# Block 1's second tile of attention: weights as two fp16 halves instead of one fp32 stationary operand

## The chip, the cores and the metric

The kernel runs on one core of one Trainium2 chip. The metric is the device time in microseconds (us) of one execution, and the median of several executions is compared. Engines are named as in the profile: PE is TensorE (PEld its weight loads), DVE is VectorE, ACT is ScalarE, POOL is GpSimd, SP is the engine that issues most of the transfers.

## The reference

One block of a small language model over 2 x 1024 tokens with a vocabulary of 128 and a width of 512, all in fp32. What matters here:

```python
h = tok(x)                                     # embedding, rms norm, projection, rms norm
h = h + attn(layernorm(h), wq, wk, wv, wo)     # 32 query heads, 8 key/value heads, head size 16, causal
h = h + ffn(layernorm(h), w_gate, w_up, w_down)   # silu(gate) * up, hidden size 2048

att = softmax(mask(q @ k.T / sqrt(16)))        # over all earlier positions
y   = att @ v
```

## The kernel before, in words

All tokens with the same id have the same query, key and value, so attention runs over the 128 ids of the vocabulary, each weighted with how often the id has been seen so far (`cT`, the counts). The 2048 tokens are 16 tiles of 128; two tiles make a block, so there are 8 blocks. A **unit** V is one tile and one key/value head group, that is 4 query heads: 8 units for a tile, 16 for a block, 128 in all. Block 1 has units 16 to 31, and its second tile has units 24 to 31.

A unit goes through these steps:

1. PE transposes two 128x128 pieces of the query rows (`turn`, L1009), and ACT (blocks 0 and 1) or DVE (later blocks) copies them to `Qst` (`stack`, L484 or L779).
2. PE computes the scores (L1020), and ACT the exponential into one of three buffers `E` (L508).
3. DVE multiplies it with the counts (L813, semaphore `w_rdy`).
4. PE multiplies with the values (`values`). The weights are the stationary operand and there are 4 of them, one for each head.

Step 4 has two forms. For V < `WIDE`, the fp32 weights in `E` are stationary against `Vf` (16 values and a one, 17 columns of fp32, L1038), two slots after the unit's scores. For V >= `WIDE`, ACT makes an fp16 copy `WTh` of the weights (L518, `wt_hi`), an engine subtracts it from the fp32 weights into the fp16 remainder `WTl` (L369 on POOL, `wt_lo`), and PE multiplies both with `Va` (high and low halves of the values and a one, 33 columns of fp16), 8 matmuls (L1044, L1045), three slots after the scores. ACT then copies two units' results out of the bank (`PVs`, L530 for the fp32 form, L533 for the fp16 form). DVE takes reciprocals of the sums (L834), and POOL multiplies (L385), in the fp16 form after adding the high and low columns (L381).

Before the change `WIDE` is 32: blocks 0 and 1 take the fp32 form, blocks 2 to 7 the fp16 form.

The order on every engine is written out by hand. `phase(n, att, ffn, m)` runs the attention of block n beside the feed-forward layer of block m = n - 1, in 24 slots. In slot s of 0 to 15, PE does `score` of unit s of the block, `turn` of unit s + 1, `values` of an earlier unit, and `gate_up(m, s)`: 24 matmuls of 256 columns (L1066 to L1068) for 128 hidden features. In slot s, ACT does `stack`, tanh of hidden piece s - 1 (L500), exp of unit s (L508), the fp16 copy of the gated piece (L512, it waits for DVE's L806), then the fp16 weight copy of unit s - 1 if there is one (L518), the copy of a finished bank, and in block 1 one `split_high`. DVE does L801 and L806 of piece s - 1, L813 of unit s, the reciprocal in odd slots, and in block 1 one `split_low`. POOL does the fp16 remainder of the gated piece (L365), and then that of the weights. In slots 16 to 23 PE does the down projection (12 matmuls of 512 columns for each slot) and between them, for each tile of the attention block, the transposes of y (L1091), the output projection `wo` (L1099 to L1101), and the transposes of the normalized rows (L1106).

Block 1 has extra work. The feed-forward weights arrive as fp32 and are split there into fp16 halves, 24 pieces in all: ACT scales and copies the high half (L475, L476), and DVE computes the low half (L752 and L754 for pieces 0 to 15, one L757 for pieces 16 to 23). PE can do `gate_up(0, s)` only when piece s is split, and the down projection of slot 16 + q only when piece 16 + q is split. These are the slots in which ACT takes its halves, and DVE takes its own one slot later:

```python
HI_NEXT = {-1: 4, 0: 5, 1: 6, 3: 7, 4: 8, 6: 9, 7: 10, 8: 11, 9: 12, 11: 13, 12: 14, 13: 15, 14: 16, 15: 17, 16: 18, 17: 19, 18: 20,
           19: 21, 20: 22, 21: 23}
SECOND_SLOTS = dict(yt=(15, 20), wo=(16, 21), ln=(17, 21), xhat=(17, 21), xn=(19, 23), fetch=(18, 22), m=(22, 3))
# PE, in gate_up:          if m == 0: pe.wait_ge(split_lo, s + 1)
# PE, down projection:     pe.wait_ge(gt_lo, 2 * q + 2); pe.wait_ge(split_lo, 16 + q + 1)
```

So DVE splits piece 11 in slot 9, 12 in slot 10, none in slot 11, 13 in slot 12, 14 in slot 13, 15 in slot 14, 16 in slot 15, 17 in slot 16 and 18 in slot 17. In slot 17 DVE also does the layer norm of the first tile (L849 to L858) before piece 18.

Of the kernel before, what the change touches and what calls it, by code (L numbers as in the profile page):

```python
# [4 lines left out]
ALU = mybir.AluOpType  # L5
# [21 lines left out]
UPB = UPT * TPB  # L27
# [7 lines left out]
MROW = 48  # L35
RING = 3
VFW = HD + 1
WIDE = 2 * UPB

EPS_RMS, EPS_LN = 1e-6, 1e-5  # L40
NEG = -3.0e38
# [26 lines left out]
def lm_block(nc, x_col, embT, emb, nw, projT, wqkv, wo, ffn_w, out, tok_tab, l_tab0, l_tab1, g_tab0, g_tab1):  # L68
    ctx = ExitStack()
    with ctx:  # L70
        def sb(name, width, dt):
            return ctx.enter_context(nc.sbuf_tensor(name, [P, width], dt))

        def sem(name):
            return ctx.enter_context(nc.semaphore(name))
# [13 lines left out]
        E = [sb(f"weights{i}", GW, F32) for i in range(RING)]  # L89
        WT = sb("weights_split", 2 * RING * GW, F16)  # L90
        WTh, WTl = ([WT[:, (2 * r + i) * GW:(2 * r + i + 1) * GW] for r in range(RING)] for i in (0, 1))
# [99 lines left out]
        def pv_bank(pair):  # L191
            return f_bank[1] if pair < UPB // 2 and pair % 2 == 1 else b_PV

        def lag(V):
            return 2 if V < WIDE else 3

# [21 lines left out]
        wt_hi, wt_lo, pv_rdy, pv_ev = (sem(n) for n in ("wt_hi", "wt_lo", "pv_ready", "pv_evacuated"))  # L218
# [69 lines left out]
        def _(pool):  # L288
# [28 lines left out]
            def fetch_rows(t):  # L317
                k = t % TPB
                if t >= TPB:
                    pool.wait_ge(h1_rdy, t - TPB + 1)  # L320
                g.indirect_dma_start(out=QG[k][:, :].bitcast(F32), out_offset=None, in_=tok_tab,  # L321
                                     in_offset=bass.IndirectOffsetOnAxis(ap=idx_x[:, t:t + 1].bitcast(U32), axis=0)
                                     ).then_inc(rows_in[k], 16)
# [13 lines left out]
            def fetch_max(t):  # L337
                pool.wait_ge(m_rdy, t - TPB + 1)
                fetch_local(t)
                fetch_group(t)  # L340
# [17 lines left out]
            def phase(n, att, ffn, m):  # L358
                at = (FIRST_SLOTS, SECOND_SLOTS, LATER_SLOTS)[min(n, 2)]
                for s in range(SLOTS):  # L360
                    if ffn and 1 <= s <= HC:
                        j = s - 1
                        i = m * HC + j
                        pool.wait_ge(gt_hi, i + 1)
                        g.tensor_tensor(gtl[:, j, :], g2[j % 2], gth[:, j, :], ALU.subtract).then_inc(gt_lo, 1)  # L365
                    if att and 1 <= s <= UPB and n * UPB + s - 1 >= WIDE:
                        V = n * UPB + s - 1
                        pool.wait_ge(wt_hi, V + 1 - WIDE)
                        g.tensor_tensor(WTl[V % RING], E[V % RING][:, :], WTh[V % RING], ALU.subtract).then_inc(wt_lo, 1)  # L369
                    if att and n > 0 and 5 <= s < UPB + 5 and s % 2 == 1:  # L370
                        k, i = divmod((s - 5) // 2, 4)
                        t = n * TPB + k
                        pool.wait_ge(pv_ev, 4 * t + i + 1)
                        if t >= TPB:
                            pool.wait_ge(yt_rdy, t - TPB + 1)
                        w = 2 * REP * PVW
                        pv = PVs[k][:, i * w:(i + 1) * w].rearrange("p (h c) -> p h c", c=PVW)
                        yv = y[k][:, i * P:(i + 1) * P].rearrange("p (h d) -> p h d", d=HD)
                        num = pv[:, :, HD:2 * HD]
                        if 8 * t + 2 * i >= WIDE:  # L380
                            g.tensor_tensor(yv, pv[:, :, 0:HD], num, ALU.add).then_inc(num_rdy, 1)  # L381
                            pool.wait_ge(num_rdy, 4 * t + i + 1 - WIDE // 2)
                            num = yv
                        pool.wait_ge(rd_rdy, 4 * t + i + 1)
                        last = g.tensor_tensor(yv, num, rden[k][:, 8 * i:8 * i + 8].unsqueeze(2).broadcast_to([P, 8, HD]), ALU.mult)  # L385
                        if i == 3:
                            last.then_inc(y_rdy, 1)
                    for k in range(TPB):
                        t = n * TPB + k
                        if att and s == at["fetch"][k] and t + TPB < TILES:  # L390
                            if t + TPB == TILES // B:
                                pool.wait_ge(g_out[1], 16)
                                for i in range(4):
                                    pool.wait_ge(l_out[1][i], 16)
                            fetch_rows(t + TPB)
                            fetch_max(t + TPB)
            phase(0, True, False, 0)
            for n in range(1, BLOCKS):
                phase(n, True, True, n - 1)
            phase(BLOCKS, False, True, BLOCKS - 1)  # L400

        @block.scalar
        def _(actq):
# [82 lines left out]
            def phase(n, att, ffn, m):  # L486
                at = (FIRST_SLOTS, SECOND_SLOTS, LATER_SLOTS)[min(n, 2)]
                for s in range(SLOTS):
# [12 lines left out]
                    if att and s < UPB:  # L501
                        V = n * UPB + s
                        actq.wait_ge(scores, V + 1)
                        if V >= WIDE + RING:
                            actq.wait_ge(wt_lo, V - RING + 1 - WIDE)
# [61 lines left out]
        def _(dve):  # L567
            v = nc.vector
# [219 lines left out]
            def phase(n, att, ffn, m):  # L788
                at = (FIRST_SLOTS, SECOND_SLOTS, LATER_SLOTS)[min(n, 2)]
                for s in range(SLOTS):  # L790
# [17 lines left out]
                    if att and s < UPB:  # L808
                        V = n * UPB + s
                        t = n * TPB + s // UPT  # L810
                        dve.wait_ge(exp_done, V + 1)
                        w = E[V % RING][:, :].rearrange("p (h n) -> p h n", h=REP)
                        v.scalar_tensor_tensor(w, w, SEEN_MAX, cT[:, t * P:(t + 1) * P].unsqueeze(1).broadcast_to([P, REP, P]),  # L813
                                               ALU.min, ALU.mult).then_inc(w_rdy, 1)
                    if n == 0 and 3 <= s < UPB + 3 and s % 2 == 1:
                        k, i = divmod((s - 3) // 2, 4)
                        pair = 4 * k + i
                        dve.wait_ge(pv_rdy, 2 * pair + 2)
                        pv = pv_bank(pair)[:, 0:2 * REP * VFW].rearrange("p (h c) -> p h c", c=VFW)
                        v.reciprocal(rden[k][:, 8 * i:8 * i + 8], pv[:, :, HD]).then_inc(rd_rdy, 1)  # L820
                        dve.wait_ge(rd_rdy, pair + 1)
                        yv = y[k][:, i * P:(i + 1) * P].rearrange("p (h d) -> p h d", d=HD)
                        v.tensor_tensor(yv, pv[:, :, 0:HD], rden[k][:, 8 * i:8 * i + 8].unsqueeze(2).broadcast_to([P, 8, HD]),
                                        ALU.mult).then_inc(pv_ev, 1)
                        if i == 3:
                            dve.wait_ge(pv_ev, pair + 1)
                            v.tensor_scalar(st[:, 25:26], rden[k][:, 0:1], 1.0, None, ALU.mult).then_inc(y_rdy, 1)
# [61 lines left out]

            place_max(0)  # L890
            phase(0, True, False, 0)
            for n in range(1, BLOCKS):
                phase(n, True, True, n - 1)
            phase(BLOCKS, False, True, BLOCKS - 1)
            store_rows(TILES - 1)

# [304 lines left out]
```

## Time and profile before

| what | value |
|---|---|
| median of 3 runs | 745.5 us (745.23 to 746.47) |
| the profiled execution: its own time | 745.95 us |
| the profiled execution: span from first to last instruction | 744.2 us |
| busy share of the span: PE, DVE, ACT, POOL | 95%, 56%, 47%, 40% |
| mean granted TensorE clock | 0.96 of full speed |

The span is the time between the first and the last instruction on the core. The profiled execution took 1.75 us more than its span. Busy shares are averages over the whole kernel; block 1's phase, in which the change lies, runs from about 113 to 206 us of the span.

### The profile page before, as it was taken

The numbers are of one execution on the slowest core, as the hardware profiler recorded it, in microseconds if no ns is written. First come the engines' busy times: TensorE is split into PE (matmuls) and PEld (weight loads), VectorE is DVE, ScalarE is ACT, GpSimd is POOL, SyncE is SP. The second block draws the span as 40 slices with busy tenths as digits, with TensorE's granted clock in tenths as the row PEclk, the third lists the DMA queues.
The fourth block names the chain that finished last, engine by engine and source line by source line (L and its number), as shares of the span: only waits on it lengthen the run. The fifth ranks groups of instructions, "written<-read, shape, count | busy, mean of one in ns | idle before, by whom it ended". The sixth has DMA issues, their size and how long they took to land.

```text
span 744.2 us, 16126 instructions
## 1 busy us (share of the span) xinstructions
PE 705.3 (95%) x6268; PEld 539.3 (72%) x6268; DVE 415.3 (56%) x1038; ACT 351.6 (47%) x722; POOL 297.9 (40%) x402
## 2 busy tenths in 40 slices
PE   7639979999899999999999999999999999999998
PEld 4429858996389847985698659964997489857873
DVE  6875387777565546545565446564655465444320
ACT  6864336775256514652266316640565046521320
POOL 7020031223137543664266516753465437530220
PEclk9955699999999999999999999999999999999999
DMA  8959020001100011001100120003000210000000
GB/s 320 411 165 346 33 89 2 1 2 45 45 30 2 2 59 60 2 2 53 66 2 3 45 73 2 3 1 102 16 2 2 72 46 2 2 15 15 2 1 28
DMA packets 10458, 40.35 MB, mean 54 GB/s; under 512 B 1808, under 2 KB 2576, under 8 KB 8592
## 3 DMA queue, kind: packets, MB, share of 16 engines
q1 hardware_dynamic: 6912, 25.44, 8.9%
q0 software_dynamic: 3328, 13.11, 5.7%
q8 instruction: 50, 0.82, 0.5%
q10 hardware_dynamic: 144, 0.79, 0.3%
q14 instruction: 24, 0.20, 0.1%
HBM read 29.89 MB, written 9.44 MB: 53 GB/s over the span
## 4 chain that ended last, share of the span: by engine, by line
PE 88%; DVE 8%; ACT 2%; issue 1%; POOL 1%; DVEq 0%; POOLq 0%
PE banks L1066 14%; PE banks L1068 14%; PE banks L1067 14%; PE banks L1150 6%; PE banks L1152 6%; PE banks L1151 6%; PE banks L1038 5%; PE banks L1020 4%; PE banks L1009 2%; PE banks L1099 2%; PE banks L1101 2%; PE banks L1100 2%; PE banks L1044 1%; PE banks L1045 1%; PE banks L1091 1%
## 5 line engine op out<-in xcount | busy, mean ns | idle before, releaser
L1068 PE MATMUL banks<-xnT_and_h,ffn_weights 128*128 128x256 f16 x1024 | 279.2, 273 | 0.0
L1067 PE MATMUL banks<-xnT_and_h,ffn_weights 128*128 128x256 f16 x1024 | 279.1, 273 | 0.0
L1066 PE MATMUL banks<-xnT_and_h,ffn_weights 128*128 128x256 f16 x1024 | 279.0, 272 | 0.0
L365 POOL TENSOR_TENSOR gated_split<-gate_work,gated_split 128x256 f16<-128x256 f32 x128 | 86.4, 675 | 269.8 <-ACT gated_split L512 269.8
L369 POOL TENSOR_TENSOR weights_split<-weights,weights_split 128x512 f16<-128x512 f32 x96 | 111.0, 1156 | 0.0
L1066 PEld LDWEIGHTS banks<-xnT_and_h,ffn_weights 128*128 128x128 f16 x1024 | 100.9, 99 | 11.4
L1068 PEld LDWEIGHTS banks<-xnT_and_h,ffn_weights 128*128 128x128 f16 x1024 | 99.9, 98 | 11.8
L1067 PEld LDWEIGHTS banks<-xnT_and_h,ffn_weights 128*128 128x128 f16 x1024 | 99.9, 98 | 11.4
L500 ACT ACTIVATE gate_work<-banks,scales 128x256 f32<-128x256 f32 x128 | 60.5, 473 | 99.9 <-PE banks L1068 99.8
L813 DVE SCALAR_TENSOR_TENSOR weights<-weights,counts_T 128x512 f32<-128x512 f32 x128 | 87.6, 685 | 25.3 <-ACT weights L508 25.1
L508 ACT ACTIVATE weights<-banks,scales 128x512 f32<-128x512 f32 x128 | 87.2, 681 | 14.1 <-PE banks L1020 14.0
L801 DVE SCALAR_TENSOR_TENSOR gate_work<-gate_work,banks 128x256 f32<-128x256 f32 x128 | 52.9, 413 | 62.1 <-ACT gate_work L500 61.9
L512 ACT ACTIVATE gated_split<-gate_work 128x256 f16<-128x256 f32 x128 | 53.4, 417 | 68.3 <-DVE gate_work L806 68.3
L779 DVE COPY q_stack<-banks 128x256 f16<-128x256 f16 x96 | 27.8, 290 | 103.1 <-PE banks L1009 103.1
L1152 PE MATMUL banks<-ffn_weights,gated_split 128*128 128x512 f16 x224 | 85.0, 379 | 0.0
L1151 PE MATMUL banks<-ffn_weights,gated_split 128*128 128x512 f16 x224 | 85.0, 379 | 0.0
L1150 PE MATMUL banks<-ffn_weights,gated_split 128*128 128x512 f16 x224 | 84.9, 379 | 0.0
L321 POOL DMA_INDIRECT token_rows<-token_table,indices x16 | 15.7, 980 | 108.5 <-DVE xnT_and_h L849 95.3
L518 ACT ACTIVATE weights_split<-weights 128x512 f16<-128x512 f32 x96 | 58.9, 613 | 0.0
L806 DVE SCALAR_TENSOR_TENSOR gate_work<-banks,gate_work 128x256 f32<-128x256 f32 x128 | 54.3, 425 | 4.4
L552 ACT ACTIVATE xnT_and_h<-banks 128x512 f16<-128x512 f32 x16 | 9.6, 597 | 83.0 <-PE banks L1106 82.4
L1020 PE MATMUL banks<-q_stack,k_stack_even 128*128 128x128 f16 x256 | 44.6, 228 | 2.4 <-ACT q_stack L484 2.4
(235 smaller groups left out, 1110.4 us busy)
## 6 DMA issues: line engine op xcount, KB each, us to landing
ffn_weights<-in_ffn_w SPq DMA_DIRECT2D x12, 1024.0 KB, 15.5
out_rows_dram<-ffn_weights SPq DMA_DIRECT2D x16, 256.0 KB, 2.0
xnT_and_h<-in_wqkv SPq DMA_DIRECT2D x1, 1536.0 KB, 8.5
local_table<-gated_split SPq DMA_DIRECT2D x2, 640.0 KB, 4.9
local_table<-xnT_and_h SPq DMA_DIRECT2D x2, 640.0 KB, 3.6
gated_split<-in_projT SPq DMA_DIRECT2D x4, 256.0 KB, 4.0
ffn_weights<-in_wo SPq DMA_DIRECT2D x1, 1024.0 KB, 10.5
token_table<-weights_split ACTq DMA_DIRECT2D x1, 768.0 KB, 8.3
```

Of the source, the lines that this page charges most:

```text
L365: g.tensor_tensor(gtl[:, j, :], g2[j % 2], gth[:, j, :], ALU.subtract).then_inc(gt_lo, 1)
L369: g.tensor_tensor(WTl[V % RING], E[V % RING][:, :], WTh[V % RING], ALU.subtract).then_inc(wt_lo, 1)
L500: a.activation(th[j % 2], f_bank[j % 3][:, 0:BLK], ACT.Tanh, scale=c_tanh).then_inc(th_rdy, 1)
L508: a.activation(E[V % RING][:, :], b_S[V % 2], ACT.Exp, scale=c_exp).then_inc(exp_done, 1)
L813: v.scalar_tensor_tensor(w, w, SEEN_MAX, cT[:, t * P:(t + 1) * P].unsqueeze(1).broadcast_to([P, REP, P]), ALU.min, ALU.mult).then_inc(w_rd ...
L1020: last = t.matmul(b_S[V % 2][:, (2 * j + a) * P:(2 * j + a + 1) * P], (KstA, KstB)[a][:, gr * P:(gr + 1) * P], Qst[:, r * 256 + j * P:r * ...
L1066: t.matmul(o, wh, xTh[m % 2][:, c, :], start=c == 0, stop=False)
L1067: t.matmul(o, wh, xTl[m % 2][:, c, :], start=False, stop=False)
L1068: last = t.matmul(o, wl, xTh[m % 2][:, c, :], start=False, stop=c == DC - 1)
L1150: t.matmul(o, hh, dn_w(j, 0), start=j == 0, stop=False)
L1151: t.matmul(o, hh, dn_w(j, 1), start=False, stop=False)
L1152: last = t.matmul(o, hl, dn_w(j, 0), start=False, stop=j == HC - 1)
```

## The change

`WIDE` becomes 24, so units 24 to 31 take the fp16 form. Their high copy is made by ACT, as in later blocks. Their remainder is made by DVE instead of POOL, placed after L813 in the slot after the unit's scores, so in slots 9 to 16 of block 1. The values of these units move from slots 10 to 17 to slots 11 to 18, the copies of their banks on ACT go from slots 11, 13, 15, 17 to slots 12, 14, 16, 18 and are 264 columns wide instead of 136, and POOL gets one addition (L381) for each pair of units.

```diff
-WIDE = 2 * UPB
+WIDE = UPB + 8
+LOW_ON_DVE = 2 * UPB
...
@@ POOL, in phase
-                    if att and 1 <= s <= UPB and n * UPB + s - 1 >= WIDE:
+                    if att and 1 <= s <= UPB and n * UPB + s - 1 >= LOW_ON_DVE:
                         V = n * UPB + s - 1
                         pool.wait_ge(wt_hi, V + 1 - WIDE)
                         g.tensor_tensor(WTl[V % RING], E[V % RING][:, :], WTh[V % RING], ALU.subtract).then_inc(wt_lo, 1)
...
@@ DVE, in phase, after L813
+                    if att and 1 <= s <= UPB and WIDE <= n * UPB + s - 1 < LOW_ON_DVE:
+                        V = n * UPB + s - 1
+                        dve.wait_ge(wt_hi, V + 1 - WIDE)
+                        v.tensor_tensor(WTl[V % RING], E[V % RING][:, :], WTh[V % RING], ALU.subtract).then_inc(wt_lo, 1)
```

## Rows read from the trace of the kernel before

**Rows 1.** Page, part 1 and part 4: busy time by engine; the chain's shares by engine.
```profile
PE 705.3 (95%) x6268; PEld 539.3 (72%) x6268; DVE 415.3 (56%) x1038; ACT 351.6 (47%) x722; POOL 297.9 (40%) x402
...
PE 88%; DVE 8%; ACT 2%; issue 1%; POOL 1%; DVEq 0%; POOLq 0%
```

**Rows 2.** Windows of block 1's later slots and of its end: us, busy, PEclk.
```profile
142.10:169.90 27.80, 27.80 (x280) 25.87 (x277) 22.57 (x39) 21.14 (x46) 6.95 (x11) 1.00 0.01 2
199.20:206.40 7.20, 7.20 (x33) 3.39 (x34) 3.18 (x6) 0.60 (x1) 0.00 (x0) 0.81 0.01 3
```

**Rows 3.** Chain that ended last, slot 10 of block 1: start us, us, what.
```profile
149.74 0.22 PE banks L1020 x4
...
150.08 0.85 PE banks L1038 x8
150.93 0.12 PE banks L1066
153.56 0.22 PE banks L1020 x4
```

**Rows 4.** Chain that ended last, slots 6 and 7 of block 2: where each begins.
```profile
224.73 0.22 PE banks L1020 x4
...
227.89 0.22 PE banks L1020 x4
```

**Rows 5.** Timeline of DVE, slots 9 to 11 of block 1.
```profile
147.08 0.42 DVE L801 SCALAR_TENSOR_TENSOR gate_work<-gate_work,banks 128x256 f32<-128x256 f32 x1 [0.53 <-ACT gate_work L500]
...
150.90 0.42 DVE L801 SCALAR_TENSOR_TENSOR gate_work<-gate_work,banks 128x256 f32<-128x256 f32 x1 [0.38 <-ACT gate_work L500]
...
151.69 0.68 DVE L813 SCALAR_TENSOR_TENSOR weights<-weights,counts_T 128x512 f32<-128x512 f32 x1
152.29 1.23 DVE L752 SCALAR_TENSOR_TENSOR ffn_weights<-ffn_weights,scales 128x512 f16<-128x512 f32 x1
153.44 0.74 DVE L754 SCALAR_TENSOR_TENSOR ffn_weights<-ffn_weights,scales 128x512 f16<-128x512 f32 x1
154.71 0.42 DVE L801 SCALAR_TENSOR_TENSOR gate_work<-gate_work,banks 128x256 f32<-128x256 f32 x1 [0.53 <-ACT gate_work L500]
```

**Rows 6.** Timelines of ACT and POOL, slots 9 and 10 of block 1.
```profile
148.48 0.71 ACT L475 ACTIVATE ffn_weights<-ffn_weights,scales 128x512 f16<-128x512 f32 x1
149.09 0.71 ACT L476 ACTIVATE ffn_weights<-ffn_weights,scales 128x512 f16<-128x512 f32 x1
150.12 0.38 ACT L484 ACTIVATE q_stack<-banks 128x256 f16<-128x256 f16 x1 [0.32 <-PE banks L1009]
150.40 0.47 ACT L500 ACTIVATE gate_work<-banks,scales 128x256 f32<-128x256 f32 x1
...
151.81 0.42 ACT L512 ACTIVATE gated_split<-gate_work 128x256 f16<-128x256 f32 x1 [0.37 <-DVE gate_work L806]
...
152.30 0.67 POOL L365 TENSOR_TENSOR gated_split<-gate_work,gated_split 128x256 f16<-128x256 f32 x1 [2.33 <-ACT gated_split L512]
```

**Rows 7.** Timeline of ACT, slot 4 of block 2.
```profile
220.47 0.61 ACT L518 ACTIVATE weights_split<-weights 128x512 f16<-128x512 f32 x1
221.00 0.37 ACT L533 ACTIVATE pv<-banks 128x264 f32<-128x264 f32 x1
```

**Rows 8.** Chain, then DVE's timeline, slots 16 to 18 of block 1.
```profile
179.00 0.80 PE banks L1038 x8
...
182.40 0.21 PE banks L1136
...
176.45 0.75 DVE L849 SCALAR_TENSOR_TENSOR xnT_and_h<-banks,scales,token_rows 128x512 f32<-128x512 f32 x1 [0.71 <-PE banks L1101]
...
180.56 2.67 DVE L757 SCALAR_TENSOR_TENSOR ffn_weights<-ffn_weights,scales 128x1024 f16<-128x1024 f32 x2
```

**Rows 9.** Timeline, then chain: PE after its wait in slot 22 of block 1.
```profile
199.20 0.58 PE L1136 MATMUL banks<-ffn_weights,gated_split 128*128 128x512 f16 x1 [2.98 <-DVE ffn_weights L757]
...
201.06 0.43 PE banks L1137
```

## The prediction

> **What bounds the kernel now.** I read the page first. PE carries 88% of the chain that ended last and is busy for 95% of the span, DVE for 56%, ACT for 47% [rows 1]. These averages invite the conclusion that moving work from PE to DVE and ACT pays. The windows view of the stage in question says otherwise: between 142 and 170 us, block 1's later slots, PE is busy all 27.8 us, but DVE 22.6 and ACT 21.1 of them [rows 2]. So next I followed one slot of that stage on each engine.
>
> On PE a slot lasts 3.82 us (149.74 to 153.56); 0.85 of it is the eight records of L1038 for one unit [rows 3]. On DVE the slot from 150.90 begins when ACT's tanh (L500) has ended, and DVE is done with piece 12 at 153.44 + 0.74 = 154.18. Then it waits 0.53 for the next tanh [rows 5]. So DVE's work fills about 3.3 of 3.82 us, and its idle time is 0.5 a slot. In ACT's slot the longest free piece is the wait of 0.3 to 0.4 for the next transposes or for L806 [rows 6]. PE is the bound here, with two followers close behind. At 3.82 us a slot they keep up, and splitting the weights (L752, L754, L757) is what they must deliver to PE in time.
>
> I number the starts of slots as PE's T (its scores) and DVE's S (its L801): T10 = 149.74, S9 = 147.08, S10 = 150.90.
>
> **What PE saves.** With values of the fp16 form a slot of block 2 takes 227.89 - 224.73 = 3.16 us [rows 4]; without any it would take 3.82 - 0.85 = 2.97 here [rows 3]. So the eight fp16 matmuls cost 0.19 and a unit saves 0.66 us: 8 x 0.66 = 5.3 us of PE's work. Moreover slot 10 has no values at all, since they move a slot later.
> The Trainium skill (TensorE: Matmul & The Clock Gate, LDWEIGHTS) prices a weight load by its columns, 128 / 1.2 = 107 ns as an estimate. By that rule eight loads would take 0.86 us and PE would save nothing, so the gain below would have no source at all. The row disagrees: the loads are hidden and the eight pairs take 0.19 us, so the sum goes by the row.
>
> **What DVE and ACT pay.** Take slot 10 as the pattern. ACT's L512 starts 0.91 after DVE's slot start (151.81 against 150.90). The fp16 weight copy comes behind it. L518 lasts 0.61 in block 2 and the next instruction can start 0.53 after it [rows 7]. L512 itself passes on after 0.32 (0.42 less the 0.1 that ACT's neighbours overlap), so the copy has ended at S + 1.84 and ACT is free at S + 1.76. The two copies of a split take 1.22 (two of 0.71, the second starts 0.61 after the first), the query stack 0.28 and the tanh 0.5. Hence ACT lets the next DVE slot start no sooner than S + 3.76, or 4.0 where a bank is copied (L533 0.37 long, 0.25 after overlap) [rows 6, 7].
>
> DVE is done with L813 at S + 1.39 (152.29). Then it must wait for the copy, until S + 1.88. The remainder itself is not in the trace as a DVE instruction. The nearest row has the same shapes (fp32 and fp16 in SBUF, fp16 out, 512 columns): L754 with 0.74, the next one starting about 0.6 later; L752 beside POOL's L365 takes 1.23 [rows 5, 6]. Nothing in it can be a gain, since it is pure addition on DVE; below I go down to 0.45, as L801 takes 0.42 for half the columns. I take 0.6, because POOL's L365 falls into the time in which DVE now waits anyway: it ran 152.30 to 152.97, and the remainder would start there, S + 2.07. That same shift spares L752 its 0.5. So: remainder until S + 2.67, the split in 1.32, and the slot lasts **4.0** instead of 3.3. In odd slots the reciprocal adds 0.1 and POOL's multiplication 0.1 to 0.2, and for the new units POOL's added L381 0.1: 4.2 and 4.3.
> The Trainium skill (SBUF — State Buffer, Who interferes with whom) says that a DVE tensor_tensor with both inputs in SBUF contends with GpSimd's reads and that the loser is blocked for the whole instruction. The 1.23 against 0.74 of L752 and L754 agrees. By that rule the remainder starts at S + 2.07, and without it at S + 1.88, which would make the sum below about 1 us smaller.
>
> **The slots one by one.** *Slots 9 to 11.* S10 = 147.08 + 4.2 = 151.3, S11 = 155.3. Slot 11 has no split on DVE, but ACT has one: it sets S12 = 155.3 + 3.76 = 159.1. PE meanwhile runs ahead, since pieces 10, 11 and 12 are ready two slots early: T11 = 149.74 + 2.97 = 152.70, T12 = 155.86, T13 = 159.02.
> *Slot 13 on PE* can start its gate and up matmuls at 159.55, but piece 13 is split in DVE's slot 12 and done at 159.1 + 4.0 = 163.1. **PE waits 3.5 us**; it had started them at 162.4 before. It ends at 165.7 (24 matmuls, 2.62); before, slot 14 began at 165.0. The saving of three slots is gone by here.
> *Slots 14 and 15.* Now each piece comes one DVE slot after the other. S13 = 163.1, piece 14 at 167.4, PE's slot 14 ends at 170.05; S14 = 167.4, piece 15 at 171.4, PE's slot 15 ends at 174.0. PE waits about 1.2 and 0.5.
> *Slots 15 and 16 on DVE.* S15 = 171.4: L813 ends at 172.8, the remainder at 174.1, the reciprocal, then y's low half (L841, at most like the remainder) at 174.85, piece 16 (L757, 1.3 each, two take 2.67 [rows 8]) at 176.15. PE's `wo` waits for 174.85, ends 2.6 later at 177.45, and PE is at slot 17 at 180.05, against 179.00 before [rows 8]. S16 = 176.15: L801 and L806 0.8, the remainder of unit 31 until 178.6, piece 17 at 179.9.
> *Slot 17 on DVE* is where the loss is sealed. The layer norm of the first tile stands before piece 18, and it took from 176.45 to 180.56, 4.1 us [rows 8]. It now starts at 180.0 and ends at 184.1, and piece 18 is done at 185.4. PE, with 0.2 and 2.6 for each of slot 17's parts, is ready for it at 183.1. It begins the down projection of slot 18 at 185.4, where it had begun it at 182.40 [rows 8]: **3.0 us late**. Behind that, DVE has slack again (no remainders), PE runs at its own pace, and the waits behind the second `wo` are unchanged and merely shifted.
>
> Edits costed at nothing: POOL's four L381 lie in its idle time (POOL is busy 7 of 27.8 us [rows 2]); the wider L533 are in ACT's 4.0; the moved values of units 26 to 31 wait for bank copies, but these come before the splits that PE waits for anyway. From block 2 on nothing changes but semaphore offsets.
>
> The sum against the profiled execution: 745.95 + 3.0; that execution is 0.45 above the median, so on the median 745.5 + 3.0 = **748.5 us**, 0.4% slower.
>
> **Bounds.** *Low:* a remainder of 0.45 with no block by POOL gives slots of 3.7 to 3.8. Then piece 13 is ready at 162.2, piece 15 at 170.0, `wo` ends at 175.6, and piece 18 at 182.85: +0.5 us. *High:* POOL blocks in every slot as for L752 (1.23), slots of 4.6: ACT's 3.76 covers slot 11, and seven slots at +0.6 give +7. *Clock:* after its wait of 2.98 us before 199.20 PE runs at half pitch, 0.43 instead of 0.215 for a matmul of 512 columns, mean granted clock 0.81 (between the levels 1.2 and 2.4 GHz) over the next 7.2 us [rows 2, 9]. That costs 7.2 x 0.19 = 1.4 us. If the shifted wait should not lower the clock, 1.4 us come back. The new wait of 3.5 us in slot 13 may lower it for the first time, but what follows it waits for DVE anyway, so less than 1 us shows.
>
> **The rivals.**
> *A, the gain arrives.* PE stays the bound and all 5.3 us come through: 740.2 us. It needs DVE slots of about 3.2 with the remainder in them. Against it: they take 3.3 already without it. Chance 0.07. It decides at piece 13: if it is ready by 159.6, this rival holds.
> *B, it cancels.* DVE is late, but nearer the low bound, or the clock does not fall after the shifted wait: from -1.5 to +1.5 us, about 746. For it: the low bound is +0.5, and the 1.4 of the clock. Chance 0.17, and 0.03 for a small gain beyond it (a cheap remainder and the clock together, about 743.5).
> *C, a greater loss.* POOL and DVE block each other in most slots, or ACT's split comes late too, so that each split waits for both: 751.5 to 753. Chance 0.10.
> *The forecast,* DVE the bound from slot 12 to slot 17, +1.5 to +5.5 us: 0.63.
>
> Differences under 0.2% (1.5 us) can't be told from no change. Faster 0.10, same 0.17, slower 0.73. The range, 745.3 to 751.5, leaves out A, the small gain, part of C and the lower half of B. The forecast's own range is 747 to 751.
>
> **What would show it.** Right: PE waits about 3.5 us on DVE's L754 before slot 13's L1066, then again before 14, 15 and slot 18; DVE's L801 are 4.0 to 4.3 apart from 147 on; the remainder is released by ACT's copy and lasts 0.65 to 0.75; ACT's idle time is gone. The last DVE wait of block 1 (before L849 of the second tile) looks as before, 3 us later. Wrong: the prediction falls if the chain in 150 to 185 us stays on PE, if L801 stay under 3.5 apart, or if the lateness at piece 18 vanishes before slot 21.

## The result, and the profile after

The changed kernel takes 748.31 us (median of 18 runs) against 745.49 us (18 runs of the kernel before beside them). The ratio is 1.0057, with a 95% interval of 1.0042 to 1.0072: slower. The prediction's 748.5 is 1.0040 of its 745.5.

The profiled execution of the changed kernel took 750.10 us, 1.8 more than the median. Of the 18 executions eleven took 747.2 to 748.7 us at a mean granted clock of 0.961 or 0.963, and seven, the profiled one among them, took 750.1 to 753.3 at 0.954 to 0.959. Where the clock fell in the others is not on record.

The page of the profiled execution, busy time and the chain's shares:

```profile
span 748.3 us, 16158 instructions
...
PE 702.7 (94%) x6268; PEld 536.9 (72%) x6268; DVE 419.5 (56%) x1046; ACT 356.3 (48%) x730; POOL 301.3 (40%) x406
...
PE 83%; DVE 11%; ACT 3%; issue 2%; DMA 1%; SPq 0%; DVEq 0%; ACTq 0%
```

PE is busy 2.6 us less than before [rows 1], in block 1 alone 3.9 less (80.81 against 84.70), and yet the span is 4.1 us longer. PE's share of the chain has fallen from 88% to 83%, and DVE's has risen from 8% to 11%.

Of those 4.1 us, 1.2 have nothing to do with the change: DVE's first L802 of block 1 (L801 before) starts at 119.74 instead of 118.56, and no instruction has changed ahead of it. In block 0 the granted clock rose later in this execution (mean 0.85 between 90 and 113 us, where it was 0.93). I therefore take 1.18 us off every time of the trace after when I compare it with the trace before. The rest, 2.9 us, arises in block 1 between slot 9 and the first scores of block 2 (210.35 against 206.24). The difference does not change after that.

The timeline of the changed kernel for slot 10 on DVE, with POOL's instruction in the same slot, answers to [rows 5, 6]:

```profile
152.36 0.41 DVE L802 SCALAR_TENSOR_TENSOR gate_work<-gate_work,banks 128x256 f32<-128x256 f32 x1
...
153.14 0.68 DVE L814 SCALAR_TENSOR_TENSOR weights<-weights,counts_T 128x512 f32<-128x512 f32 x1
154.23 0.75 DVE L819 TENSOR_TENSOR weights_split<-weights,weights_split 128x512 f16<-128x512 f32 x1 [0.41 <-ACT weights_split L519]
154.90 0.74 DVE L753 SCALAR_TENSOR_TENSOR ffn_weights<-ffn_weights,scales 128x512 f16<-128x512 f32 x1
155.56 0.74 DVE L755 SCALAR_TENSOR_TENSOR ffn_weights<-ffn_weights,scales 128x512 f16<-128x512 f32 x1
156.22 0.41 DVE L802 SCALAR_TENSOR_TENSOR gate_work<-gate_work,banks 128x256 f32<-128x256 f32 x1
...
153.75 0.67 POOL L366 TENSOR_TENSOR gated_split<-gate_work,gated_split 128x256 f16<-128x256 f32 x1 [1.86 <-ACT gated_split L513]
```

The slot takes 156.22 - 152.36 = 3.86 us; 4.0 was forecast. DVE waits 0.41 for ACT's copy, the remainder (L819) takes 0.75 and passes on after 0.67, and POOL's L366 runs while DVE waits, so L753 takes 0.74 and not 1.23. There is no idle time before the next L802, where there had been 0.53.

The chain that ended last, through slot 13 (start us, us, what):

```profile
157.03 0.24 PE banks L1025 x4
...
157.52 0.44 issue
157.96 0.71 ACT ffn_weights L476
158.67 0.61 ACT ffn_weights L477
159.28 0.27 ACT q_stack L485
159.55 0.37 ACT gate_work L501
159.94 0.43 DVE gate_work L802
160.40 0.43 DVE gate_work L807
...
161.18 0.62 ACT weights_split L519
...
161.86 0.63 issue
162.49 0.74 DVE ffn_weights L753
163.23 0.67 DVE ffn_weights L755
163.90 0.14 issue
164.04 0.27 PE banks L1071
```

This is the stretch that the prediction worked out. Up to slot 12 the chain lies on PE; there ACT's two copies, the stack and the tanh set when DVE's slot begins, and ACT's weight copy, the remainder and the split of piece 13 follow one another until PE can start slot 13. Who waited for whom, between 120 and 210 us (us in total, times, longest):

```profile
PE banks L1141 <- DVE ffn_weights L758: 5.4, 2, 3.0
...
DVE weights_split L819 <- ACT weights_split L519: 3.8, 8, 1.0
...
PE banks L1071 <- DVE ffn_weights L755: 2.6, 2, 1.5
...
PE banks L1049 <- ACT pv L534: 1.6, 1, 1.6
```

PE's wait in slot 13 is shown in two parts, 3.2 us together: 1.6 in which the values of unit 26 wait for a bank to be copied, and 1.55 for piece 13. Slots 15 and 18 wait 1.06 and 2.46 for a piece, slot 14 not at all (the forecast had 1.2 there and 0.5 before slot 15); the 2.98 of slot 22 are still there.

The steps, with 1.18 taken off the measured times:

| step | before | predicted | measured |
|---|---|---|---|
| DVE's slot 10 starts | 150.90 | 151.3 | 151.18 |
| DVE's slot 11 | 154.71 | 155.3 | 155.04 |
| DVE's slot 12 | 158.53 | 159.1 | 158.76 |
| PE's gate and up matmuls of slot 13 start | 162.23 | 163.1 | 162.86 |
| DVE's slot 14 | 166.17 | 167.4 | 168.45 |
| y's low half is done | 172.1 | 174.85 | 175.62 |
| PE's down projection of slot 18 starts | 182.40 | 185.4 | 186.48 |
| first scores of block 2 | 206.24 | 209.24 | 209.17 |

The forecast is within 0.35 us up to slot 13, then 1.05 too early, and right again at the end. Both deviations go back to the granted clock. Two windows of the trace after (PEclk is the third number from the end):

```profile
160.00:164.00 4.00, 0.89 (x16) 0.60 (x14) 3.50 (x7) 3.63 (x9) 0.67 (x1) 1.00 0.01 2
165.00:168.40 3.40, 3.40 (x21) 2.54 (x20) 2.85 (x5) 2.04 (x4) 2.27 (x3) 0.53 0.02 5
```

After a stretch in which PE is busy 0.89 of 4 us, the clock falls to its lower level (1.2 GHz), and slot 13's matmuls start 0.21 us apart instead of 0.11. The tanh behind them comes late, and DVE waits 1.37 us before its slot 14. In the trace before, the clock fell in slot 22 instead [rows 2, 9]. Here it does not fall there:

```profile
204.62 0.38 PE banks L1141
205.00 0.22 PE banks L1142
```

### The profile page after: what moved, and what is told of

The parts are those of the page before. It is cut to its first block, busy times and chain, and to the rows that moved or that the text cites. A ratio compares the mean times of both kernels' runs of the same rounds, so it can differ in the third digit from the quotient of the medians.

```text
span 748.3 us, 16158 instructions
## 1 busy us (share of the span) xinstructions
PE 702.7 (94%) x6268; PEld 536.9 (72%) x6268; DVE 419.5 (56%) x1046; ACT 356.3 (48%) x730; POOL 301.3 (40%) x406
## 4 chain that ended last, share of the span: by engine, by line
PE 83%; DVE 11%; ACT 3%; issue 2%; DMA 1%; SPq 0%; DVEq 0%; ACTq 0%
PE banks L1071 14%; PE banks L1073 14%; PE banks L1072 14%; PE banks L1155 6%; PE banks L1157 6%; PE banks L1156 6%; PE banks L1025 4%; PE banks L1043 4%; PE banks L1014 2%; PE banks L1104 2%; PE banks L1105 2%; PE banks L1106 2%; PE banks L1049 1%; PE banks L1050 1%; PE banks L1096 1%
## 5 line engine op out<-in xcount | busy, mean ns | idle before, releaser
L366 POOL TENSOR_TENSOR gated_split<-gate_work,gated_split 128x256 f16<-128x256 f32 x128 | 86.0, 672 | 267.8 <-ACT gated_split L513 267.8
L370 POOL TENSOR_TENSOR weights_split<-weights,weights_split 128x512 f16<-128x512 f32 x96 | 111.1, 1157 | 0.0
L814 DVE SCALAR_TENSOR_TENSOR weights<-weights,counts_T 128x512 f32<-128x512 f32 x128 | 87.7, 686 | 25.5 <-ACT weights L509 25.4
L802 DVE SCALAR_TENSOR_TENSOR gate_work<-gate_work,banks 128x256 f32<-128x256 f32 x128 | 52.9, 413 | 60.2 <-ACT gate_work L501 59.9
L519 ACT ACTIVATE weights_split<-weights 128x512 f16<-128x512 f32 x104 | 63.8, 614 | 0.0
```

Of the source, the lines that this page charges most:

```text
L519: a.activation(WTh[V % RING], E[V % RING][:, :], ACT.Copy).then_inc(wt_hi, 1)
```

## The experiments

Each ratio is to runs of the kernel before on the same chip, with 6 to 12 executions of the kernel in question; experiments one to four, five to eight and nine to twelve ran on three different chips.

**One. The remainder back on POOL.** `LOW_ON_DVE = UPB + 8` in place of `2 * UPB`.

> The changed kernel with one thing put back: the remainder of units 24 to 31 is computed by POOL (L369's place, 1.16 us each in block 2) instead of DVE. Theory D (DVE's slot is the bound, and POOL and DVE block each other on operands in SBUF): the 1.16 of POOL falls between the halves of DVE's weight split, DVE's slots of 12 to 16 become about 4.5 us instead of 4.0, and the kernel is 2 to 4 us slower than the changed one, 1.008 to 1.012 of before. Rival F (POOL works beside DVE for free): DVE's slots go back to about 3.3 to 3.8, only ACT's copy is left of the cost, and the kernel is at 0.998 to 1.002 of before.

Measured: 1.0069 (1.0050 to 1.0087). Rival F falls. The cost is less than theory D said, about what DVE's own remainder costs. The timeline of slot 12:

```profile
159.89 1.23 DVE L753 SCALAR_TENSOR_TENSOR ffn_weights<-ffn_weights,scales 128x512 f16<-128x512 f32 x1
159.90 0.67 POOL L366 TENSOR_TENSOR gated_split<-gate_work,gated_split 128x256 f16<-128x256 f32 x1 [1.58 <-ACT gated_split L513]
160.53 1.60 POOL L370 TENSOR_TENSOR weights_split<-weights,weights_split 128x512 f16<-128x512 f32 x1
...
161.04 1.64 DVE L755 SCALAR_TENSOR_TENSOR ffn_weights<-ffn_weights,scales 128x512 f16<-128x512 f32 x1
```

POOL's remainder and DVE's L755 run at the same time and both are long: 1.60 instead of 1.16, 1.64 instead of 0.74. DVE's slot 12 takes 4.11 us (158.49 to 162.60), where 4.5 was expected. POOL idles three quarters of the time, yet its work costs DVE about as much as DVE's own: from slot 9 to slot 16 DVE takes 30.16 us, against 29.67 in the changed kernel.

DVE's slots are not the whole of this kernel's loss. In its trace PE does not wait for piece 18 any more, since slot 16 on DVE is short without a remainder, but the clock fell twice in block 1, after the waits of slots 13 and 22, where it fell once in the changed kernel. Block 1 takes 90.46 us against 90.61, so without the second fall it would be the shorter of the two.

**Two to four. The two costs taken away one by one.** The copy and the remainder of units 24 to 31 are cut to 8 of 512 columns: the remainder in experiment two, the copy in three, both in four (the diff). These kernels leave out the rest of what PE should multiply with. The buffers are filled once in block 0.

```diff
-v.tensor_tensor(WTl[V % RING], E[V % RING][:, :], WTh[V % RING], ALU.subtract).then_inc(wt_lo, 1)
+v.tensor_tensor(WTl[V % RING][:, 0:8], E[V % RING][:, 0:8], WTh[V % RING][:, 0:8], ALU.subtract).then_inc(wt_lo, 1)
...
-a.activation(WTh[V % RING], E[V % RING][:, :], ACT.Copy).then_inc(wt_hi, 1)
+w = GW if V >= LOW_ON_DVE else 8
+a.activation(WTh[V % RING][:, 0:w], E[V % RING][:, 0:w], ACT.Copy).then_inc(wt_hi, 1)
```

> The remainder on DVE covers 8 columns instead of 512, so the low half that PE multiplies with is not the remainder; ACT's copy stays whole. (The buffer is filled once in block 0, so that nothing undefined is read.) Theory D: DVE's slots shrink from 4.0 to 3.4 to 3.5, and ACT's path (next tanh no sooner than 3.76 to 4.0 after DVE's slot start) is left as the bound; about 2 us of the loss go, 1.000 to 1.003 of before. Rival A (ACT's copy alone is the cost, DVE has room): the time stays that of the changed kernel, 1.005 to 1.006.

Measured: 1.0003 (0.9991 to 1.0015). Without most of the remainder nearly the whole loss is gone; rival A falls. But 1.4 us of this may be the clock, which did not fall in block 1 of this trace, in spite of a wait of 1.5 us before slot 18 and of 2.98 before slot 22:

```profile
181.00:206.00 25.00, 21.82 (x121) 11.60 (x122) 15.12 (x31) 7.58 (x12) 3.64 (x5) 1.00 0.16 50
```

Block 1, from DVE's first L801 (L802) to the first scores of block 2, takes 87.68 us in the kernel before, 90.61 in the changed one and 86.66 here. Less a half clock of about 1.4 us in the first two, that is 86.3, 89.2 and 86.7, so by this estimate 2.5 of the 2.9 us are the remainder's.

> ACT's fp16 copy of units 24 to 31 covers 8 columns instead of 512; DVE's remainder stays 512 wide, so both halves are not what they should be. Theory D: ACT's path is 0.5 us shorter, but DVE's remainder now starts behind L813 and meets POOL's L366 (0.67), so DVE's slot stays at about 3.9 to 4.0; only slot 12, which ACT sets, starts 0.5 to 0.9 earlier; 0.5 to 1 us come back, 1.004 to 1.005 of before. Rival A (ACT's copy is the cost): nearly all comes back, 1.000 or less.

Measured: 1.0034 (1.0020 to 1.0048), a little more back than expected, though the interval reaches the expected 1.004 to 1.005. DVE's slot stays long for the reason given: the remainder now starts behind the multiplication and runs beside POOL.

```profile
153.55 0.67 POOL L368 TENSOR_TENSOR gated_split<-gate_work,gated_split 128x256 f16<-128x256 f32 x1 [1.86 <-ACT gated_split L515]
153.60 1.16 DVE L826 TENSOR_TENSOR weights_split<-weights,weights_split 128x512 f16<-128x512 f32 x1
```

> Both: ACT's copy and DVE's remainder cover 8 columns each, so only PE's side of the change is left (fp16 matmuls, values one slot later). Theory D: PE's 5.3 us are real, and DVE's slots of 3.4 let most of them through: 3 to 4.5 us faster than before, 0.994 to 0.996. Rival P (the fp16 form does not free PE, since eight weight loads cost what four fp32 ones do): the same time as before or more.

Measured: 1.0009 (0.9996 to 1.0022). My theory was wrong here: nothing of PE's 5.3 us came through. One reason is that DVE's cost was not all but gone. The 8 columns still take DVE 0.6 us, since they too meet POOL:

```profile
158.82 0.67 POOL L368 TENSOR_TENSOR gated_split<-gate_work,gated_split 128x256 f16<-128x256 f32 x1 [1.93 <-ACT gated_split L515]
158.88 0.64 DVE L826 TENSOR_TENSOR weights_split<-weights,weights_split 128x8 f16<-128x8 f32 x1
```

L758 behind it takes 0.74 in place of 1.23, so DVE's slot is no longer than before. DVE's slots 12 to 15 start at 157.41, 161.01, 164.92 and 168.34. In slots 13 and 15, in which the reciprocal and either POOL's work beside it or y's low half are added, DVE's own work takes 3.9 and 4.0 us, and from slot 13 until slot 16 DVE waits for nobody:

```profile
161.01 0.42 DVE L807 SCALAR_TENSOR_TENSOR gate_work<-gate_work,banks 128x256 f32<-128x256 f32 x1 [0.17 <-ACT gate_work L503]
...
163.99 0.89 DVE L760 SCALAR_TENSOR_TENSOR ffn_weights<-ffn_weights,scales 128x512 f16<-128x512 f32 x1
164.92 0.42 DVE L807 SCALAR_TENSOR_TENSOR gate_work<-gate_work,banks 128x256 f32<-128x256 f32 x1
```

PE meanwhile waits 1.44, 0.72, 1.71 and 2.98 us for pieces 13, 14, 18 and 22. From piece 13 on each piece is split only one slot before its use, so PE can run no further ahead than DVE lets it. I read this as a loop over three engines (piece 13, slot 13's matmuls, tanh, DVE's slot 14, piece 15: 7.5 us for two slots), and the chain does pass that way once. But DVE's slot 14 would have started at 164.9 without it, as its own work ended at 164.88. So what experiment four shows is the late pieces, and not that the loop sets DVE's pace. The new theory, L: the pieces' lead decides whether anything PE saves is worth something.

**Five to seven. The pieces one slot earlier.**

```diff
-HI_NEXT = {..., 9: 12, 11: 13, 12: 14, 13: 15, 14: 16, 15: 17, 16: 18, 17: 19, 18: 20, 19: 21, 20: 22, 21: 23}
+HI_NEXT = {..., 9: 12, 10: 13, 11: 14, 12: 15, 13: 16, 14: 17, 15: 18, 16: 19, 17: 20, 18: 21, 19: 22, 20: 23}
```

> The kernel before, with weight pieces 13 to 23 split one slot earlier (ACT takes piece 13 in its free slot 10, piece 23 in slot 20; DVE one slot later each). Theory L (a piece that is split only one slot before PE needs it is what ties the three engines together): PE is the bound in slots 9 to 16 here, so nothing moves there; but piece 22 is now done before the second tile's layer norm, so the 2.98 us wait before slot 22's down projection goes, and the half clock behind it where it falls: 3 to 4.4 us faster, 0.994 to 0.996 of before. Rival N (that wait has another cause behind it, such as the layer norm itself): within 0.1% of before.

Measured, in the kernel before: 0.9968 (0.9953 to 0.9983), 2.4 us and so a little less than the 3 to 4.4 expected. The 2.98 us wait of slot 22 is gone, and from slot 2 to slot 22 the timeline shows no wait of PE for another engine. The wait stood in the kernel before all along [rows 9]: piece 22 was queued behind the second layer norm. The clock does not fall in block 1 of this trace, which takes 84.0 us in place of 87.7; about 1.4 of the difference is the clock.

> The changed kernel with the same earlier pieces. Theory L: PE no longer waits for a piece before slots 13 to 15 and 18, but y's low half in DVE's slot 15 comes as late as in the changed kernel, since DVE's slots stay at 4.0 us; the start of slot 18's down projection is some 0.5 us later than in the kernel before instead of 4, and the 2.98 us wait goes too: 0.994 to 0.997 of before, not faster than the kernel before with the same shift. Rival N: the waits move to other semaphores and it stays at 1.003 to 1.006.

Measured, in the changed kernel: 0.9976 (0.9961 to 0.9991), just outside the expected 0.994 to 0.997, and as expected no faster than experiment five. No PE wait for a piece is left. PE now waits, with the values of units 26 and 28, for banks that ACT copies late, as its slots lag behind PE's:

```profile
PE banks L1049 <- ACT pv L534: 3.9, 2, 2.0
```

> ACT's copy and DVE's remainder of units 24 to 31 cover 8 columns each, and the pieces are split one slot earlier. Theory L: this is the case in which PE's saving can come through, since neither the work of the followers nor the late pieces hold it; about 4 us more than the kernel before with early pieces, 0.987 to 0.990 of before. Rival P (the fp16 form gives PE nothing): 0.994 to 0.996, the same as the kernel before with early pieces.

Measured, with both costs cut to 8 columns: 0.9923 (0.9900 to 0.9945). Against experiment five that is 0.0045, or 3.4 us, of the 5.3 that PE saves; about 4 were expected, and the interval still touches rival P's 0.994. The traces decide: neither has a fall of the clock in block 1, which takes 81.24 us against 83.97, and PE is busy 78.73 us of it against 83.40. So the saving is real (rival P falls). They also say what brought it through. From slot 9 to slot 16 DVE takes 25.38 us here and 25.38 in experiment four: its pace has not changed, and the loop did not set it. What has changed is that PE no longer waits for a piece; it waits 0.99 us for a bank and 0.73 for y's low half.

**Eight. PE kept busy in its wait.**

```diff
@@ PE, behind the values, before the wait for the piece
+                if m == 0 and s == 13:
+                    for _ in range(7):
+                        t.matmul(f_bank[1], id16[:, :], cT[:, 0:512], start=True, stop=True)
...
@@ PE, before the values
+                    if ffn and m == 0 and s == 13:
+                        pe.wait_ge(g2_rdy, 11)
+                        for _ in range(7):
+                            t.matmul(f_bank[1], id16[:, :], cT[:, 0:512], start=True, stop=True)
```

> The changed kernel with 14 matmuls of 512 columns into an idle bank in slot 13 of block 1, seven before and seven after the values, while PE waits there (1.60 and 1.55 us). They compute nothing that is used. If the half clock after this wait is a term of the loss, the granted clock stays at full speed in slots 13 and 14, DVE's wait of 1.37 us before its slot 14 shrinks to under 0.5, and about 1 us comes back: 1.003 to 1.005 of before. If the clock does not matter there: 1.0055 or more, since the added matmuls can only delay.

Measured: 1.0059 (1.0037 to 1.0081): nothing came back, though the interval is wide enough for 1.5 us. Yet the first half happened as expected. Slot 13 ran at the full clock, DVE had no wait before slot 14, and slot 18 began 1.5 us earlier than in the changed kernel, counted from the first L802 of block 1 (66.45 us after it instead of 67.92). But now the clock fell at that later wait:

```profile
183.53 0.58 PE L1148 MATMUL banks<-ffn_weights,gated_split 128*128 128x512 f16 x1 [2.46 <-DVE ffn_weights L758]
183.91 0.63 PE L1149 MATMUL banks<-ffn_weights,gated_split 128*128 128x512 f16 x1
184.33 0.63 PE L1150 MATMUL banks<-ffn_weights,gated_split 128*128 128x512 f16 x1
```

```profile
162.00:170.00 8.00, 6.68 (x77) 5.88 (x76) 7.12 (x14) 6.87 (x14) 2.94 (x4) 1.00 0.00 1
183.00:187.00 4.00, 3.47 (x10) 1.31 (x11) 1.79 (x3) 1.33 (x2) 1.10 (x2) 0.57 0.04 11
```

In these three traces one long wait each pays for the clock (slot 22 before, slot 13 after, slot 18 here), and each time it costs about 1.4 us by my estimate. The other traces show that this is no rule. In block 1 the clock fell not at all in experiment two, twice in one and three times in twelve; it fell after a wait of 2.20 us in eleven and after waits of 2.01 and 1.86 in six, and not after those of 2.97 and 2.98 before slot 22 in two, three, eight, eleven and the changed kernel. So which wait pays is decided by something other than its length alone, and what that is stays open. A difference of 1.4 us between two single traces can be the clock.

**Nine and ten. Fewer units, with early pieces.** `WIDE = UPB + 12` and `WIDE = UPB + 14`.

> The changed kernel with early pieces and WIDE at UPB + 12, so that only units 28 to 31 take the fp16 form. DVE's remainders fall into slots 13 to 16. Theory D: y's low half in slot 15 is then about as late as PE needs it (PE's three saved values are spent waiting for it), and only the two values behind the output projection are a gain: 1 to 2 us faster than the kernel before with early pieces (0.9968), so 0.994 to 0.996 of before. Rival S (each fp16 unit saves its 0.66 us wherever it is): 0.993. Rival W (any remainder on DVE in block 1 costs more than it brings): 0.997 or more.

> The same with WIDE at UPB + 14: units 30 and 31 alone take the fp16 form. Their remainders fall into slots 15 and 16, where DVE keeps some slack once the pieces come early, and their values into PE's slots 17 and 18. Theory D: both savings come through, 1.3 us less than with early pieces alone, 0.994 to 0.996 of before, the same as with four units. Rival W: 0.997 or more.

Measured: 0.9944 (0.9925 to 0.9964) and 0.9944 (0.9925 to 0.9962), as theory D had it. With four units PE waits 1.85 us for y's low half before the output projection; with two the timeline shows no wait from slot 2 to slot 22. Block 1, from DVE's first L802 to block 2's scores, takes 83.4 and 82.8 us, against 84.0 in experiment five, all three without a fall of the clock, and 87.7 with one before. These are the fastest of the kernels here that compute everything, 4 us under the kernel before.

**Eleven. The remainder behind the split**, at the end of DVE's slot.

> The changed kernel with DVE's remainder moved behind the weight split at the end of its slot. DVE no longer waits for ACT's copy, but its split now meets POOL's L366, so the slot should take 3.95 us instead of 4.0, while each piece is ready about 0.6 us earlier in its slot. Theory D (DVE's sum of work sets the end of the stage, at the layer norm before piece 18): only 0.3 to 1 us comes back, 1.0045 to 1.0055 of before. Rival J (it is the lateness of each piece within its slot): 2 us or more come back, 1.003 or less.

Measured: 1.0041 (1.0024 to 1.0058), between the two; rival J's 1.003 and the changed kernel's 1.0057 are both inside the interval, so this run alone excludes neither. DVE's slots 10 to 12 take 3.80, 3.72 and 4.02 us. So the slots are as long as in the changed kernel (3.86 in slot 10), as theory D said, and PE's wait before slot 18 is 2.20 us instead of 2.46.

**Twelve. The remainder twice**, once into an unused buffer.

> The changed kernel with each of the eight remainders computed twice, once more into an unused buffer. Theory D (DVE bound): 8 x 0.67 = 5.3 us more work, of which slot 11 hides some 0.7 to 1: 4 to 5 us slower than the changed kernel, 1.011 to 1.0125 of before. Rival A (ACT's chain of 3.76 to 4.0 us sets the slots): the second computation hides partly behind it, 1.006 to 1.009.

Measured: 1.0111 (1.0088 to 1.0134). Eight more remainders of 0.67 us, 5.3 in all, cost (1.0111 - 1.0057) x 745 = 4.0 us. DVE's slot 10 takes 4.46 us, 0.6 more than the 3.86 of the changed kernel. ACT's chain hides little of it. In this trace the clock fell three times in block 1, which takes 97.50 us; less two falls of 1.4 that is 4.1 more than in the changed kernel.

## Why the prediction was right

*The bound of the stage.* Right. PE was the bound in block 1 with two followers close behind, and the change turned the order round. Experiments two and twelve show it from both sides: with 8 columns of the remainder the loss is gone (1.0003, up to 1.4 us of it by the clock), and with two remainders it nearly doubles (1.0111).

*DVE's slot.* Forecast 4.0, measured 3.86. The remainder cost 0.67 until the next instruction, 0.6 was taken. The split behind it took 1.32, as forecast, because POOL's L366 fell into DVE's wait. The remainder started at S + 1.87 and not at S + 2.07: in slot 10 at 154.23, while L366 ran until 154.42. It took 0.75; the second one of experiment twelve, with nothing beside it, takes 0.68.
The rule of the Trainium skill (SBUF — State Buffer, Who interferes with whom), that the loser is blocked for the whole instruction, agrees with the traces, but only behind a start of 0.1 to 0.2 us that does overlap. The remainder ended 0.56 us after L366. In slot 12 of experiment one L753 ended 0.55 after L366 (161.12), POOL's L370 1.01 after L753 (162.13), and L755 0.55 after L370 (162.68), where they last 0.74, 1.16 and 0.74 alone; the 8 columns of experiment four ended 0.03 after L368. So each ends as if it had waited for the other and then run all but its start. The 4.5 us that I expected of that slot, against 4.11 measured, were too long by my sum and not by the rule.

*ACT's path.* Right in slot 12: 3.76 forecast, 3.72 measured (156.22 to 159.94). It set one slot only. Experiment three says what ACT's copy costs by itself: 1.0057 to 1.0034, 1.7 us, though the intervals of the two overlap and they ran on different chips.

*PE's saving.* The unit's 0.66 us is right: seen in 3.15 us for a slot with fp16 values (153.88 to 157.03), as in [rows 4]. That the saving was "gone by slot 13" is right as well. What I did not see is that more than the remainder stood in its way: in experiment four PE still waits 3.9 us for pieces 13, 14 and 18, which the kernel before does not, and with the pieces one slot earlier, at the same pace of DVE, 2.7 of the 5.3 us show in block 1 (81.24 in experiment seven against 83.97 in five). Rival A was given 0.07 on the ground that DVE's slots took 3.3 already. The late pieces are a second ground.

*The late piece 18.* Right in mechanism; 185.4 forecast, 186.48 measured. The layer norm in slot 17 stood before it, and PE waited 2.46 us. Two figures on the way were off: slot 13's matmuls had started at 162.23 before and not at 162.4, and by the prediction's own times the wait before slot 15 would have been 0.8 and not 0.5.

*The clock.* This step failed, in both directions, and that the two errors cancelled is luck. I wrote that the half clock in slot 13 would show as less than 1 us, "since what follows it waits for DVE anyway". It cost 1.4 us at DVE's slot 14 (5.67 us after slot 13, against 4.23 in experiment eight, which avoided it and was 1.5 us earlier at slot 18), because from slot 13 on DVE's tanh waits for PE too. And I left the half clock of slot 22 in the sum (though I kept its 1.4 us in the range), where it did not occur in this execution. Without either, block 1 of the changed kernel is about 2.8 us longer than before, near the forecast's 3.0 (86.3 against 89.1 us, each less its own half clock of 1.4 to 1.5).

*The size.* The ratio of 1.0057 stands for 4.2 us (3.1 to 5.4), the two medians differ by 2.8, and the two traces by 2.9 after the start of block 1. The forecast of 3.0 (1.0040) is just below the ratio's interval. Single executions differ in the clock of block 0 and, as the experiments show, of block 1, and I have only one trace of each kernel, the changed one's from an execution 1.8 us above its median; so this is left open.

## What to carry to other kernels

Before moving work off the engine that is always busy, measure the followers' slack in that stage and in that slot (here 0.5 us a slot against 0.66 saved and 1.1 added with its wait), not over the whole span. Then ask how far ahead the followers deliver: while pieces were split only one slot before their use, nothing of what PE saved showed (experiment four), and one more slot of lead was worth 0.3% here in the kernel before, without any of the change. Once the lead was there, the change for the last two units alone shortened block 1 by another 1.2 us (82.8 against 84.0 us; 0.9944 against 0.9968, with intervals that overlap). And before a difference of one or two us between two traces is explained, compare their granted clock: here one fall more or less is 1.4 us.

## What the runs showed of the hardware

A DVE subtraction with both operands in SBUF that meets a POOL instruction reading SBUF ends as if it had waited for that instruction's end and overlapped only its own first 0.1 to 0.2 us. One of 8 columns took 0.57 to 0.64 us where it started with a POOL instruction of 0.67 (experiment four) and 0.22 where it started 0.2 before its end (experiment two); one of 512 columns took 0.68 alone and 1.16 beside it (experiment three). In the reverse direction a POOL subtraction of 512 columns took 1.60 us in place of 1.16 behind a DVE instruction that had started before it (experiment one).

The granted clock fell to its lower level after PE waits of 2.20 us (experiment eleven), 2.46 (three and eight), 2.98 (before and four) and 3.2 in two parts (after), and stayed at the upper one after waits of 2.97 or 2.98 us before slot 22 in five traces (two, three, eight, eleven and after). Filling one wait with unused matmuls kept the clock up there, and it fell at the next long wait; nothing was gained.
